# Two quarters of a shared feed-forward placed behind the experts' tiles, and output in four equal chunks

## What is computed

```
x = x + xattn(layernorm(x), ctx_1024)          # cross attention over 1601 keys, then a layer norm
x = x + attn(layernorm(x))                     # attention with 17 pooled positions
x = x + ffn(layernorm(x))                      # the part that the change touches

# ffn, per token (flat = layernorm(x), 2048 x 256):
topk_scores, topk_idx = top_k(flat @ router_w.T + router_bias, 2)   # 16 experts
topk_scores = softmax(topk_scores)
hidden = silu(gate_all) * up_all               # of the chosen experts, 128 wide
out = sum over the two of score * (hidden @ down_proj)
sh_hidden = silu(flat @ sh_gate.T) * (flat @ sh_up.T)               # shared, 256 wide
out = out + sh_hidden @ sh_down.T
```

## Time and profile before

| | us |
|---|---|
| median of 3 timed runs | 566.16 |
| lowest and highest of them | 564.48 and 569.11 |
| span of the profiled execution (first to last instruction) | 577.5 |

### The profile page before, as it was taken

How to read it: one execution, slowest core, us unless ns; L and a number is a source line. 1 busy time by engine, 2 the same in 40 slices (tenths; PEclk the granted TensorE clock), 3 DMA queues, 4 the chain that set the end, 5 groups by cost and what they waited for, 6 DMA issues and landing times.

```text
span 577.5 us, 14401 instructions
## 1 busy us (share of the span) xinstructions
PE 506.9 (88%) x4952; PEld 346.8 (60%) x4953; DVE 395.7 (69%) x1038; ACT 191.1 (33%) x589; POOL 198.2 (34%) x302
## 2 busy tenths in 40 slices
PE   7997999999999999999989999998941999999900
PEld 7674656566666666666546666665520577887700
DVE  3798798999989999995536777778510234555525
ACT  2334323233333333333124455443100034555400
POOL 3002213211111221222145667551776015555520
PEclk9999999999999999999979999999985899999965
DMA  7999678797987988831289566200232124444258
GB/s 282 359 299 336 194 210 252 261 303 265 292 279 267 287 279 276 281 108 38 56 241 268 172 191 207 65 1 2 84 108 101 38 76 127 135 139 134 76 166 270
DMA packets 67296, 108.65 MB, mean 188 GB/s; under 512 B 8195, under 2 KB 49077, under 8 KB 67256
## 3 DMA queue, kind: packets, MB, share of 16 engines
q1 hardware_dynamic: 60840, 97.70, 54.1%
q0 software_dynamic: 3792, 8.43, 4.2%
q10 hardware_dynamic: 2624, 1.97, 1.1%
HBM read 85.31 MB, written 24.72 MB: 191 GB/s over the span
## 4 chain that ended last, share of the span: by engine, by line
PE 76%; DMA 6%; issue 6%; DVE 5%; ACT 4%; SPq 1%; POOL 1%; ACTq 0%; POOLq 0%; DVEq 0%
PE banks L1065 15%; PE banks L1041 14%; PE banks L1424 7%; PE banks L1322 4%; DMA ring<-in_ctx_dram 4%; PE banks L1436 3%; PE banks L1213 3%; PE banks L1053 3%; PE banks L1379 3%; PE banks L1078 3%; PE banks L1000 2%; DVE ctxT L1529 2%; PE banks L1418 2%; PE banks L1181 2%; PE banks L1174 2%
## 5 line engine op out<-in xcount | busy, mean ns | idle before, releaser
L1529 DVE STREAM_TRANSPOSE ctxT<-ring 128x832 f32<-128x832 f32 x128 | 121.8, 1010 | 4.2 <-DMA ring<-in_ctx_dram 4.2
L1041 PE MATMUL banks<-ctxT,qT_all 32*64 32x416 f32 (+2 forms) x2048 | 93.0, 498 | 2.1 <-issue 1.2
L1065 PE MATMUL banks<-ring,prob 128*64 128x256 f32 (+1 forms) x832 | 93.6, 381 | 0.7 <-ACT prob L795 0.7
L1065 PEld LDWEIGHTS banks<-ring,prob 128*64 128x64 f32 (+1 forms) x832 | 58.5, 137 | 31.6 <-issue 4.2
L1041 PEld LDWEIGHTS banks<-ctxT,qT_all 32*64 32x64 f32 x2048 | 56.6, 131 | 30.1 <-issue 13.2
L717 POOL DMA_INDIRECT expert_out<-prob,dest x47 | 46.2, 984 | 60.7 <-DVE prob L1892 40.3
L611 POOL TENSOR_TENSOR var<-mv,eps 128x1 f32<-128x1 f32 x32 | 6.3, 196 | 167.6 <-DVE mv L1574 115.5
L808 ACT ACTIVATE prob<-banks,negmax 128x416 f32<-128x416 f32 (+2 forms) x80 | 41.3, 533 | 30.3 <-DVE negmax L1551 30.3
L1424 PE MATMUL banks<-ring,ctxT 128*128 x188 | 48.9, 382 | 0.4 <-ACT ctxT L919 0.4
L1885 DVE TENSOR_TENSOR ctxT<-banks,ctxT 128x128 f32<-128x128 f32 x47 | 13.7, 292 | 41.0 <-ACT ctxT L922 30.8
L647 POOL TENSOR_TENSOR ctxT<-ctxT,k_mask 128x1088 f32<-128x1088 f32 x16 | 33.1, 2068 | 25.2 <-ACT ctxT L873 25.2
(11 more groups left out here) (245 smaller groups left out, 907.1 us busy)
## 6 DMA issues: line engine op xcount, KB each, us to landing
ring<-in_ctx_dram SPq DMA_DIRECT2D x48, 1024.0 KB
qT_all<-q_by_pair SPq DMA_DIRECT2D x56, 128.0 KB, 8.9
ctxT<-rows_by_expert SPq DMA_DIRECT2D x47, 129.0 KB
rows_by_expert<-blank SPq DMA_DIRECT2D x12, 387.0 KB, 4.3
mid<-stage SPq DMA_DIRECT2D x31, 128.0 KB, 2.3
ring<-in_ctx_dram SPq DMA_DIRECT2D x16, 130.0 KB
ctxT<-mid SPq DMA_DIRECT2D x16, 128.0 KB, 2.3
qT_all<-mid SPq DMA_DIRECT2D x16, 128.0 KB, 2.5
```

The source lines that it names most:

```text
L1041: last = pe.matmul(S[a][64 * b:64 * b + 64, 0:KW[a]], q_rep[mine, r, c, 64 * b:64 * b + 64], ctxT[mine, c, b, 0:KW[a]], start=c == 0, stop ...
L1065: last = pe.matmul(U[64 * b:64 * b + 64, 0:D], probT[0:rows, k, 64 * b:64 * b + 64], ring[0:rows, r, b, k, :], start=k == 0, stop=k == KT)
L1529: dve.transpose(ctxT[:, c].rearrange("p b (k j) -> p (b k) j", j=Q), ring[:, r].rearrange("p b k c -> p (b k) c")[:, :, columns(c):columns ...
```

## The change

The shared work of quarters 2 and 3 (LATE = 2) leaves its place ahead of the experts' tiles. TensorE now starts the tiles when shared_added is 8. Both gate halves of quarter 2 stand between the last tile's second turn (L1430) and its down product (L1436); the rest of the shared work follows behind that product. On VectorE hidden(2) stands behind the last tile's result, hidden(3) behind the first chunk's results, and the adds of quarter 2 and quarter 3 behind the results of chunks 2 and 3. The chunks are now four groups each, so that a chunk is a quarter, and the last two are written out when their shared adds are done.

```diff
--- before.py
+++ after.py
@@ -45,7 +45,8 @@
     Q_SCALE = float(DV) ** -0.5
     NG = TOK // P
     GB = P // NL
-    CHUNKS = (4, 5, 5, 2)
+    CHUNKS = (4, 4, 4, 4)
+    LATE = 2
     ROWS = 4
     KV_RING = 4
     HG = 6
@@ -549,7 +550,10 @@
                         .then_inc(y_loaded[n], 16)
             for n, size in enumerate(CHUNKS):
                 first = sum(CHUNKS[:n])
-                sp.wait_ge(mixed_ready, TOPK * (n + 1))
+                if n < LATE:
+                    sp.wait_ge(mixed_ready, TOPK * (n + 1))
+                else:
+                    sp.wait_ge(shared_added, 4 * (n + 1))
                 for q in range(GB):
                     sp.dma_start(out.rearrange("l (g q) c -> q l g c", q=GB)[q][:, first:first + size, :],
                                  x2_all[NL * q:NL * q + NL, first:first + size, :]).then_inc(written, 16)
@@ -905,12 +909,15 @@
             act.wait_ge(gap_ready, 1)
             act.activation(gap_e[:, :], gap_w[:, :], ACT.Exp).then_inc(gap_exp, 1)
 
-            for q in range(4):
+            def shared_gates(q):
                 for hc in range(DH):
                     act.wait_ge(shared_up_done, 2 * DH * q + hc + 1)
                     if q >= 1:
                         act.wait_ge(shared_hid_ready, DH * (q - 1) + hc + 1)
                     act.activation(sh_silu[:, hc, :], bank[1 + hc][:, :], ACT.Silu).then_inc(shared_silu, 1)
+
+            for q in range(LATE):
+                shared_gates(q)
 
             def turn(s, p, ahead=True, back1=True):
 
@@ -934,6 +941,8 @@
             for s in range(SLOTS // 2 * 2, SLOTS + 2):
                 turn(s, s % 2, s < SLOTS, s < SLOTS + 1)
                 hidden_out(s - 2, s % 2)
+            for q in range(LATE, 4):
+                shared_gates(q)
 
 
         @block.tensor
@@ -1388,10 +1397,10 @@
                 .then_inc(before_done, 1)
             shared_half(0, 1, 0)
             shared_half(0, 1, 1)
-            for q in range(1, 4):
+            for q in range(1, LATE):
                 shared_up(q)
                 shared_down(q - 1)
-            shared_down(3)
+            shared_down(LATE - 1)
 
             expert_now = [pe.alloc_register(f"expert_now{r}") for r in range(ROWS)]
             expert_old = [pe.alloc_register(f"expert_old{r}") for r in range(2)]
@@ -1451,7 +1460,7 @@
 
             pe.wait_ge(expert_step, 4)
             pe.wait_ge(experts_loaded, 16 * 3 * NE)
-            pe.wait_ge(shared_added, NG)
+            pe.wait_ge(shared_added, 4 * LATE)
             pe.wait_ge(place_ready, 2)
             for s in range(ROWS):
                 turn(s, s, 0, True, s >= 1, s >= 2, s >= 3, False)
@@ -1463,8 +1472,18 @@
                 experts = next_experts(it)
                 for r in range(ROWS):
                     turn(it * ROWS + r, r, it, experts=experts)
-            for s in range(SLOTS // ROWS * ROWS, SLOTS + 3):
+            for s in range(SLOTS // ROWS * ROWS, SLOTS + 2):
                 turn(s, s % ROWS, s // ROWS, s < SLOTS, s < SLOTS + 1, s < SLOTS + 2)
+            shared_half(LATE, 0, 0)
+            shared_half(LATE, 0, 1)
+            back(SLOTS - 1, (SLOTS - 1) % 2, expert_of(SLOTS - 1))
+            shared_half(LATE, 1, 0)
+            shared_half(LATE, 1, 1)
+            pe.wait_ge(y_ready, SLOTS)
+            for q in range(LATE + 1, 4):
+                shared_up(q)
+                shared_down(q - 1)
+            shared_down(3)
 
 
         @block.vector
@@ -1868,10 +1887,10 @@
             dve.tensor_scalar(expert_m[:, :], expert_f[:, :], float(NE - 1), None, ALU.min).then_inc(expert_step, 1)
             dve.wait_ge(expert_step, 3)
             dve.tensor_copy(experts_i[:, 1:SLOTS + 2], expert_m[:, :]).then_inc(expert_step, 1)
-            for q in range(2, 4):
+            for q in range(2, LATE):
                 shared_hidden(q)
                 shared_add(q - 1)
-            shared_add(3)
+            shared_add(LATE - 1)
 
 
 
@@ -1915,14 +1934,29 @@
                 result(s - 3, (s - 3) % ROWS, (s - 3) // ROWS)
 
 
-            for n, size in enumerate(CHUNKS):
+            def results_added(n):
                 first = sum(CHUNKS[:n])
                 dve.wait_ge(y_loaded[n], 16 * TOPK)
-                rows = slice(first, first + size)
+                rows = slice(first, first + CHUNKS[n])
+                dve.wait_ge(shared_added, 4 * min(n, LATE - 1) + 4)
                 for k in range(TOPK):
                     if k:
                         dve.wait_ge(mixed_ready, TOPK * n + k)
                     dve.tensor_tensor(x2_all[:, rows, :], y_all[k][:, rows, :], x2_all[:, rows, :], ALU.add).then_inc(mixed_ready, 1)
+
+            def shared_last(q):
+
+                dve.wait_ge(mixed_ready, TOPK * q + TOPK)
+                shared_add(q)
+
+            shared_hidden(LATE)
+            results_added(0)
+            shared_hidden(LATE + 1)
+            results_added(1)
+            results_added(2)
+            shared_last(2)
+            results_added(3)
+            shared_last(3)
 
 
 # ---- launch: one core; inputs and outputs as the reference has them ----
```

## The result

| | before | after |
|---|---|---|
| timed median, us | 566.98 (4 runs, 564.48 to 569.11) | 576.89 (4 runs, 575.14 to 578.91) |
| span of the profiled execution, us | 577.5 | 573.4 |

What follows compares the result with a forecast made beforehand. TensorE was taken to bound the tiles, with the shared work ahead of them already hidden behind the scatter in timed runs. Front 0 plus tail 9.4 on the median 566.2 gave 575.6 us, range 561.5 to 578.5.

Steps and rivals of the forecast that it cites:

- The stall: TensorE's waits ahead of the tiles, 13.72 us and a second until 447.4 us in the profile; claimed absent in timed runs.
- The sum that made it look exact: Span without TensorE's waits ahead of the tiles, 577.5 - 15.7 = 561.8, plus 4.4 us around it: 566.2, the timed median.
- The page on the launch: Rule putting a profile's total about 6.2 us above reported time; not counted; if applied, 5.1 us of the difference left.
- The case of a real stall: TensorE's wait ahead of the tiles also in timed runs: tiles start 15.7 us earlier, -12.7 after the lower clock's cost.
- Front 0, bounds 0 to 3: Ahead of the tiles, moving shared work away gains 0 us, as tiles wait for rows; at most 3 us gain.
- The late send, +2.9: In the tail, two gate halves ahead of the last down product delay the last send and every result load 2.9 us.
- VectorE's chain: In the tail, VectorE paced by its own adds and four waits for TensorE's products (3.5 to 7 us), ending at 582.9.
- The sign of a granted clock of 0.5 "between 566 and 573": In the tail of the new profile, TensorE's granted clock was to be 0.5 between 566 and 573 us.
- Tail +9.4: After the last tile, the span's end moves from 577.5 to 586.9, +9.4 us; +10.9 at the lower clock throughout.
- the even chunks as about +1: In the tail, the larger last chunk's two adds cost 2 x 1.23 us for 2 x 0.7 before; about +1 us.
- Rival 1: TensorE's wait ahead of the tiles is real in timed runs: -12.7 there, +9.4 in the tail, 562.9 us; chance 0.22.

## Why the prediction was right, point by point

- **The stall was absent in timed runs: right.** Four things carry it: a second profile without it, 20.7 us of work taken away for nothing, 8.6 us added for nothing, and 21.5 us added for the price of what lies beyond the slack. What was argued from two numbers (a span 11.3 us above the timed median, signals late with no sender) is shown by these for the timed runs as a whole.
- **The sum that made it look exact was luckier than it was good.** I had 561.8 us of span and 4.4 us around it. In fact 1.7 us lie around a span. The sum also left out that without the stall the tiles begin at the lower clock: their stage took 83.4 us in the first profile, and 85.2 in the second. 561.8 + 1.8 + 1.7 = 565.3. The two errors, 1.8 and -2.7, nearly cancel, and that 561.8 + 4.4 met the median of 566.2 was luck.
- **The page on the launch** ("Runtime: NRT & Kernel Launch" of the Trainium skill, section "The ~15µs preamble/postamble breakdown") gives 6.2 us between a profile's total and the reported time. Spans as used here don't hold that part: the reported time was 1.7 us above the span, not below it. The case of a real stall, which that rule would have fed, fell.
- **Front 0, bounds 0 to 3: right.** The lower bound of 3 us rested on a scatter that is faster untraced. Profiles can't tell that, and both have about the same pitch, (444.9 - 405.4)/31 = 1.27 us in the first and (445.2 - 404.9)/31 = 1.30 in the second, but the timed runs with the work left out show no gain, with 1.3 us inside their interval at most.
- **The late send, +2.9:** the loads start 7.75 us behind the last second turn (536.01 to 543.76) for 5.10 in the earlier trace rows (549.01 to 554.11): +2.65. Taken away, it gave 2.2.
- **VectorE's chain:** predicted to end at 582.9 on the clock of before, 33.9 us behind the last second turn. Measured 33.45. Groups 10 and 11 waited at the lower clock, 1.83 and 1.29 us; groups 14 and 15 at the full clock, 0.89 and 0.44, as the lower of my two values had it. The sign of a granted clock of 0.5 "between 566 and 573" is 553 to 560 on the clock of after: there it was 0.95 from 553.5 to 555.0 and 0.50 from then on. The writes behind the last add took 3.95 us for the 4.0 of the sum.
- **Tail +9.4:** the profile of after has 37.4 us and its repeat 37.0; the five with the old tail 27.8 on average. That is +9.4, and the timed medians differ by 9.9 in one session and by 8.6 in the other, where the ratio of 1.017 makes it 9.5. Part of the match is luck: against the single tail of before from which the sum was made (28.5) the profile of after has +8.9. One term in it had the wrong sign: I had counted the even chunks as about +1, and they are -1 (26.7 for 27.8 in the profiles; 0.9955 timed). The forecast of VectorE's end does not hang on it, as the chain of after was summed as a whole. Against that tail of 26.7 the changed one is 10.7 longer: 2.2 for the gate halves, 5.7 for the two banks (4.8 of them at the adds), and 3.3 that stay with both mended (30.0 - 26.7), of which the eight adds are 2.8, twice 1.41. The three make 11.2, half a microsecond more than measured.
- **Rival 1** priced the start at the lower clock at 3 us. It is 1.6. Its time would have been 561.5, and the case had fallen anyway.
- **What stays open:** what held TensorE's signals back in the first profile. It was one profile in six of those whose shared work goes on beside the scatter. Whether it ever happens to a timed run isn't known. The timed runs of the kernel before spread from 560.92 to 574.41 us; the start of the scatter alone moves by 7 us between profiles, and a part-stall in the longest of them can't be excluded. No run here tells whether the recording caused it.

## What to carry to other kernels

Before a stall in a profile is worth an edit, compare the execution's own time with the timed median: where it is longer by about the length of the stall, take a second profile, or leave the work out and time it. Work is hidden if taking it away changes nothing; work that is hidden ahead of a stage is only moved onto the path when it is put behind it. When work is moved into a tail that one engine's chain sets, count every wait that few buffers force between the two engines: here the two banks cost 4.8 us of a tail that grew by 9.4, 1.8 of them because TensorE had waited so long that its clock was down, and one bank per product gave it back.

## What the runs showed of the hardware that I had not expected

A stall can sit in one profile of a program and not in the next. The earlier trace rows show its first piece, 13.72 us of TensorE, and a second brings it to the first tile's start 60.2 us behind the scatter's; in the second profile that is 44.9 us. The tiles began 15.8 us later on the span's clock and were 1.8 us shorter, being started at the full clock, which makes the 13.9 us by which the two spans differ.
